# GpSimd clears 32 instead of 128 columns of `iota_i` behind each paced row gather

## The chip, the cores and the metric

One core of a Trainium2 chip runs the whole program in one launch. The metric is device time in microseconds (us). TensorE is called PE in the profile, its weight loads PEld, VectorE is DVE, ScalarE is ACT, GpSimd is POOL, and SP is the engine that only issues DMAs.

## The reference, cut to what matters

Two layers over `x` (16 sequences of 256 tokens of 256 features). Layer 0 is an attention and a feed-forward net of 8 experts, of which each token takes one. Layer 1 is a mixture of 8 small experts, of which each token takes two, plus a shared expert; then a second gated layer, in which each sequence takes two experts of 8:

```
y_all = einsum('etm,emh->eth', gp * up, w_down)        # every expert for every token
y_sel = y_all[topk_idx, arange(T)[:, None], :]         # the two that the token chose
y     = (y_sel * topk_w[..., None]).sum(1) + p         # p: the shared expert
...
pooled = y.mean(axis=1); logits = pooled @ gate_w.T + gate_b      # one set per sequence
gates  = softmax(two highest logits)
out    = x + sum over the two experts of gates * gelu(y @ expert_w.T + expert_b)
```

The kernel computes only the experts that were chosen. It sorts the 2 x 4096 (token, choice) pairs by expert into 71 tiles of 128 rows, runs each tile through its expert, writes the results to `y2_sorted` in HBM in sorted order, and then fetches for each token its two result rows.

## The kernel before, in words

The program runs in stages, and each engine has its own instruction stream; they meet at semaphores. Rows are fetched by index with `gather_rows` (line 886): GpSimd executes an indirect DMA (DMA_INDIRECT in the profile) that fetches 128 rows of 1 KB into a tile of SBUF. All gathers are GpSimd's, in the order of its stream.

Behind some gathers stands `space()` (lines 913 to 916): GpSimd clears the tile `iota_i` (128 partitions x 128 int32; it was read long before, at the start, by lines 1940 and 1941, and isn't read again), raises the semaphore `paced` and waits for it. Such a gather is called paced here. With these inputs they are:

- 16 gathers of `y_late` in `expert_rows` (lines 918 to 925), which bring layer 0's expert results to `add_rows` on VectorE (line 2563); TensorE works on the shared expert of layer 1 meanwhile (lines 1412 and 1422)
- the first 6 of the 71 gathers of `choice_rows` (lines 946 to 951), which bring the tokens of the sorted tiles. From the fourth on each also waits until TensorE has turned the tile three before it (`c_g`). TensorE turns tile `i` at line 1485 and runs it through its expert at lines 1493, 1501 and 1507
- the 64 gathers of the last stage (lines 959 to 965): four for each sequence `b` (two halves of its 256 tokens, two choices), into `yk[b % 3]`. Before the four of sequence `b` GpSimd waits until VectorE has summed sequence `b - 3` (`d_z`)

What follows in the last stage, for each sequence: VectorE sums the shared expert's row and the two fetched ones (`sum_choices`, line 2695, four instructions for a sequence, which need all four gathers landed); TensorE turns the sum (`turn_z`, line 1538); ScalarE copies it out (line 1874); TensorE makes the gate's logits (line 1546); VectorE finds the two experts (lines 2704 to 2710); TensorE runs them (lines 1553 and 1559); ScalarE applies the gelu (line 1887); VectorE adds the two results with their gates (`weigh`, line 2727, one instruction for each expert); SP stores. The order is written out by hand: in `gated_step(b)` TensorE turns `z` of `b`, works on the experts of `b - 1` around the logits of `b`, and starts on `b`'s first expert. VectorE takes the gate of `b`, the first `weigh` of `b - 1`, the sum of `b + 1`, and then the second `weigh` of `b - 1`.

Of the kernel before, what the change touches and what calls it, by code (L numbers as in the profile page):

```python
# [3 lines left out]
def bass_adaln_ffn_kernel(  # L4
# [18 lines left out]
    P = 128  # L23
# [36 lines left out]
    with ctx:  # L60
        def sb(name, shape, dt=F32):
            return ctx.enter_context(nc.sbuf_tensor(name, shape, dt))

        def sem(name):
            return ctx.enter_context(nc.semaphore(name))
# [26 lines left out]
        iota_i = sb("iota_i", [P, P], I32)  # L92
# [461 lines left out]
        paced = sem("paced")  # L554
# [242 lines left out]
        def _(pool):  # L797
# [114 lines left out]

            def space():
                spaced[0] += 1
                pool.memset(iota_i[:, :], 0).then_inc(paced, 1)  # L915
                pool.wait_ge(paced, spaced[0])

            def expert_rows(rows, first):
                for i in range(first, NC):
                    c = UNIT_CHUNKS[i]  # L920
                    if i >= first + NU:
                        pool.wait_ge(a_x1, i - NU + 1)
                    gather_rows(yg[i % NU], rows, pos_i[:, c:c + 1], a_got[i % NU // 4])
                    if first:
                        space()
# [20 lines left out]
            def choice_rows(i):  # L946
                if i >= RT:
                    pool.wait_ge(c_g, i - RT + 1)
                gather_rows(c_gath[i % RT], x1_dram, row_tok2[:, i:i + 1], c_got[i % RT])
                if i < 2 * RT:  # L950
                    space()
# [7 lines left out]
            for b in range(B):  # L959
                if b >= RT:  # L960
                    pool.wait_ge(d_z, b - RT + 1)
                for n in range(NB):
                    for k in range(2):
                        gather_rows(yk[b % RT][:, 2 * n + k, :], y2_dram, pos_k_i[:, b * NB + n, k:k + 1], d_got[b % RT])
                        space()
# [1901 lines left out]
```

## Time and profile before

| | us |
|---|---|
| median of 3 runs (lowest to highest) | 617.16 (613.28 to 618.48) |
| the profiled execution, whole | 610.94 |
| its span | 609.1 |
| busy: PE / PEld / DVE / ACT / POOL | 537.2 / 456.9 / 324.4 / 232.0 / 245.1 |
| DMA_INDIRECT of line 886, last stage (x64) | 64.6 |
| MEMSET of line 915 (x86) | 18.8 |

The span runs from the first to the last instruction of one profiled execution; whatever lies around it makes up the 1.84 us to that execution's own time. A busy share says how long an engine executed, not whether anybody waited for it. Whether an engine sets the time in a stretch is read from the chain that ended last and from the waits. Instructions of an engine are listed with start and duration; an "idle before" names what released the instruction. In every stretch that matters here TensorE had its full clock, 2.4 GHz (PEclk 1.00).

### The profile page before, as it was taken

The numbers are of one execution on the slowest core, as the hardware profiler recorded it, in microseconds if no ns is written. First come the engines' busy times: TensorE is split into PE (matmuls) and PEld (weight loads), VectorE is DVE, ScalarE is ACT, GpSimd is POOL, SyncE is SP. The second block draws the span as 40 slices with busy tenths as digits, with TensorE's granted clock in tenths as the row PEclk, the third lists the DMA queues.
The fourth block names the chain that finished last, engine by engine and source line by source line (L and its number), as shares of the span: only waits on it lengthen the run. The fifth ranks groups of instructions, "written<-read, shape, count | busy, mean of one in ns | idle before, by whom it ended". The sixth has DMA issues, their size and how long they took to land.

```text
span 609.1 us, 11343 instructions
## 1 busy us (share of the span) xinstructions
PE 537.2 (88%) x3716; PEld 456.9 (75%) x3716; DVE 324.4 (53%) x970; ACT 232.0 (38%) x651; POOL 245.1 (40%) x394
## 2 busy tenths in 40 slices
PE   0499999772499999999999999999999988988885
PEld 0478888661499999998878887888888877756564
DVE  3567667749322332772527934444444444655655
ACT  0145445550011111114554335555555454433342
POOL 6313113004211112103835446555555157877860
PEclk9999999995599999999999999999999999999999
DMA  7960000059496552341469004565656423555552
GB/s 169 357 278 2 2 2 1 2 207 415 156 341 222 181 174 53 106 136 48 93 203 300 1 25 132 157 162 154 161 154 159 112 71 121 182 158 179 166 181 72
DMA packets 53204, 88.27 MB, mean 145 GB/s; under 512 B 11250, under 2 KB 43891, under 8 KB 51604
## 3 DMA queue, kind: packets, MB, share of 16 engines
q1 hardware_dynamic: 45028, 65.29, 30.8%
q0 software_dynamic: 8112, 22.16, 15.3%
q8 instruction: 36, 0.59, 0.4%
q14 instruction: 28, 0.23, 0.1%
HBM read 62.38 MB, written 25.04 MB: 144 GB/s over the span
## 4 chain that ended last, share of the span: by engine, by line
PE 67%; POOL 13%; issue 6%; DVE 6%; DMA 5%; ACT 1%; SPq 0%; DVEq 0%; POOLq 0%; ACTq 0%
POOL arena L886 10%; PE psum L1257 10%; PE psum L1268 9%; PE psum L1493 8%; PE psum L1412 7%; PE psum L1132 5%; PE psum L1104 5%; PE psum L1507 5%; PE psum L1422 3%; DMA arena<-x,row_tok 3%; PE psum L1485 2%; POOL iota_i L915 2%; PE psum L1112 2%; PE psum L1440 1%; PE psum L1126 1%
## 5 line engine op out<-in xcount | busy, mean ns | idle before, releaser
L886 POOL DMA_INDIRECT arena<-x,row_tok x71 | 68.1, 959 | 51.3 <-PE psum L1485 44.2
L886 POOL DMA_INDIRECT arena<-y_sorted,pos_k_i x64 | 64.6, 1010 | 36.1 <-POOL iota_i L915 18.6
L1493 PE MATMUL psum<-big_w,arena 128*128 x284 | 72.9, 379 | 0.0
L1257 PEld LDWEIGHTS psum<-arena,big_w 128*128 128x128 f32 x512 | 61.4, 197 | 2.8 <-issue 1.2
L1257 PE MATMUL psum<-arena,big_w 128*128 128x128 f32 x512 | 61.8, 281 | 1.5 <-DVE arena L2441 1.5
L1559 PE MATMUL psum<-big_w,arena 128*128 x256 | 62.9, 379 | 0.0
L1780 ACT ACTIVATE arena<-psum,arena 128x128 f32<-128x128 f32 x64 | 18.2, 368 | 117.3 <-PE psum L1257 117.3
L1412 PE MATMUL psum<-arena,big_w 128*128 128x256 f32 x256 | 60.0, 381 | 0.0
L1493 PEld LDWEIGHTS psum<-big_w,arena 128*128 128x128 f32 x284 | 53.7, 190 | 7.2
L1268 PE MATMUL psum<-arena 128*128 128x256 f32 (+1 forms) x256 | 57.7, 379 | 0.0
L2678 DVE SCALAR_TENSOR_TENSOR arena<-arena 128x128 f32<-128x128 f32 x71 | 20.8, 293 | 60.7 <-ACT arena L1866 60.7
L1412 PEld LDWEIGHTS psum<-arena,big_w 128*128 128x128 f32 x256 | 47.1, 191 | 6.5 <-issue 0.4
L1268 PEld LDWEIGHTS psum<-arena 128*128 128x128 f32 x256 | 47.5, 190 | 5.8
L1559 PEld LDWEIGHTS psum<-big_w,arena 128*128 128x128 f32 x256 | 46.6, 189 | 5.6
L886 POOL DMA_INDIRECT arena<-h_late,row_tok x16 | 15.4, 960 | 85.2 <-PE psum L1245 72.7
L874 POOL TENSOR_TENSOR arena<-arena 128x512 f32<-128x512 f32 x16 | 19.0, 1189 | 65.0 <-DVE arena L2064 65.0
L1507 PE MATMUL psum<-big_w,arena 128*128 x142 | 44.0, 392 | 0.7 <-ACT arena L1863 0.7
L2695 DVE SCALAR_TENSOR_TENSOR arena<-arena,w_k 128x256 f32<-128x256 f32 x64 | 28.2, 481 | 13.1 <-issue 7.9
L1863 ACT COPY arena<-psum 128x256 f32<-128x256 f32 x71 | 26.4, 372 | 22.0 <-PE psum L1507 22.0
L1132 PE MATMUL psum<-arena 128*128 128x256 f32 x144 | 32.7, 380 | 1.6 <-ACT arena L1674 1.6
L1104 PE MATMUL psum<-arena 128*128 128x128 f32 x256 | 31.8, 285 | 0.3 <-DVE arena L2064 0.3
L1422 PE MATMUL psum<-big_w,arena 128*128 128x256 f32 x128 | 30.6, 382 | 1.3 <-ACT arena L1803 1.3
(320 smaller groups left out, 970.4 us busy)
## 6 DMA issues: line engine op xcount, KB each, us to landing
y_sorted<-arena SPq DMA_DIRECT2D x71, 128.0 KB, 2.6
big_w<-w SPq DMA_DIRECT2D x8, 1024.0 KB, 4.9
tokens<-x SPq DMA_DIRECT2D x4, 1024.0 KB, 14.0
x<-tokens SPq DMA_DIRECT2D x16, 256.0 KB, 2.9
z_kept<-arena SPq DMA_DIRECT2D x16, 256.0 KB, 3.1
out<-arena SPq DMA_DIRECT2D x16, 256.0 KB, 2.5
y_late<-arena SPq DMA_DIRECT2D x16, 128.0 KB, 1.7
big_w<-expert_w_t SPq DMA_DIRECT2D x1, 2048.0 KB, 7.6
```

Source lines behind the costliest of these rows:

```text
L886: pool.indirect_dma_start(dst, None, rows, bass.IndirectOffsetOnAxis(ap=idx, axis=0)).then_inc(done, 16)
L1104: mm = pe.matmul(bank[a][:, (j % 4) * P:(j % 4 + 1) * P], wq_s[:, k, j * P:(j + 1) * P], xt_l[:, k, :], start=k == 0, stop=k == KD - 1)
L1132: mm = pe.matmul(bank[6][:, 0:D], lhs(j), wo_s[:, j, :], start=j == 0, stop=j == NPAIR - 1)
L1257: mm = pe.matmul(bank[1 + 2 * u + f // 4][:, (f % 4) * P:(f % 4 + 1) * P], big_w[:, c:c + P], g_t[:, k, :], start=k == 0, stop=k == KD - 1)
L1268: mm = pe.matmul(bank[5 + j % 2][:, 0:D], act_t[j % 2][:, f, :], arena[:, bass.ds(e * (NF * D) + f * D, D)], start=f == 0, stop=f == NF - 1)
L1412: mm = pe.matmul(bank[up_bank(b) + q][:, half * S:(half + 1) * S], w[:, k, q * M1:(q + 1) * M1], p_s[:, unit(b)[1][k], :], start=k == 0, s ...
L1422: mm = pe.matmul(bank[6][:, n * D:(n + 1) * D], mid[u][q][:, n * P:(n + 1) * P], md_s[:, E1 + q, :], start=q == 0, stop=q == NSH - 1)
L1493: mm = pe.matmul(bank[2 + i % RT][:, 0:2 * M1], c_gt[i % RT][:, k, :], mgu_s[:, k, bass.ds(e, 1), :].rearrange("p a m -> p (a m)"), start= ...
L1507: pe.matmul(bank[5][:, 0:D], c_midt[i % RT], md_s[:, bass.ds(e, 1), :].rearrange("p a d -> p (a d)"), start=True, stop=True).then_inc(c_dn, 1)
L1559: mm = pe.matmul(o, z_t[u][:, k, n * P:(n + 1) * P], ew_s[:, k, bass.ds(e, 1), :].rearrange("p a d -> p (a d)"), start=False, stop=n == NB ...
L1863: act.copy(c_y[t % RT], bank[5][:, 0:D]).then_inc(c_yc, 1)
L2695: m = dve.scalar_tensor_tensor(z_s[u][:, n, :], yk[u][:, 2 * n + k, :], w_k[:, k, bass.ds(b * NB + n, 1)], base, ALU.mult, ALU.add)
```

## The change

`space()` clears the first `P // 4` = 32 columns of `iota_i` on all 128 partitions, not all 128 columns. The number of gathers, of clears, of semaphore steps and waits stays as it was; nothing else is changed.

```diff
             def space():
                 spaced[0] += 1
-                pool.memset(iota_i[:, :], 0).then_inc(paced, 1)
+                pool.memset(iota_i[:, 0:P // 4], 0).then_inc(paced, 1)
                 pool.wait_ge(paced, spaced[0])
```

## Rows read from the trace of the kernel before

**Rows 1.** The page: span, and the chain that ended last, by engine and line.
```profile
span 609.1 us, 11343 instructions
...
PE 67%; POOL 13%; issue 6%; DVE 6%; DMA 5%; ACT 1%; SPq 0%; DVEq 0%; POOLq 0%; ACTq 0%
POOL arena L886 10%; PE psum L1257 10%; PE psum L1268 9%; PE psum L1493 8%; PE psum L1412 7%; PE psum L1132 5%; PE psum L1104 5%; PE psum L1507 5%; PE psum L1422 3%; DMA arena<-x,row_tok 3%; PE psum L1485 2%; POOL iota_i L915 2%; PE psum L1112 2%; PE psum L1440 1%; PE psum L1126 1%
```

**Rows 2.** Busy time by stretch: start:end, length, engines' busy us, PEclk, DMA share, GB/s.
```profile
283.00:307.00 24.00, 24.00 (x156) 19.99 (x155) 10.37 (x27) 15.10 (x39) 18.97 (x32) 1.00 0.39 86
...
369.50:475.00 105.50, 105.13 (x571) 89.02 (x571) 49.15 (x189) 60.98 (x190) 60.98 (x64) 1.00 0.59 158
492.00:590.00 98.00, 85.21 (x425) 64.90 (x424) 58.10 (x183) 40.77 (x132) 77.54 (x127) 1.00 0.51 154
```

**Rows 3.** The chain that ended last, its end: start, us, what.
```profile
589.60 3.24 DMA arena<-y_sorted,pos_k_i
...
593.90 0.89 DVE arena L2695 x2
```

**Rows 4.** POOL's instructions in order of time, last stage: start, us, instruction, [idle before].
```profile
492.21 0.94 POOL L886 DMA_INDIRECT arena<-y_sorted,pos_k_i  x1 [15.93 <-DMA y_sorted<-arena]
...
522.34 1.15 POOL L886 DMA_INDIRECT arena<-y_sorted,pos_k_i  x1 [0.27 <-POOL iota_i L915]
...
531.03 1.46 POOL L886 DMA_INDIRECT arena<-y_sorted,pos_k_i  x1 [0.52 <-POOL iota_i L915]
...
536.38 0.95 POOL L886 DMA_INDIRECT arena<-y_sorted,pos_k_i  x1 [0.27 <-POOL iota_i L915]
...
573.37 0.95 POOL L886 DMA_INDIRECT arena<-y_sorted,pos_k_i  x1 [0.27 <-POOL iota_i L915]
574.32 0.22 POOL L915 MEMSET iota_i<- 128x128 int32 x1
574.81 0.95 POOL L886 DMA_INDIRECT arena<-y_sorted,pos_k_i  x1 [0.27 <-POOL iota_i L915]
...
583.70 1.04 POOL L886 DMA_INDIRECT arena<-y_sorted,pos_k_i  x1 [0.27 <-POOL iota_i L915]
...
589.60 1.21 POOL L886 DMA_INDIRECT arena<-y_sorted,pos_k_i  x1 [0.27 <-POOL iota_i L915]
```

**Rows 5.** POOL's groups by shape: line, operation, shape, count | busy us, mean ns | idle.
```profile
L915 POOL MEMSET iota_i<- 128x128 int32 x86 | 18.8, 218 | 0.1
...
L813 POOL MEMSET units<- 128x8 int32 x70 | 2.5, 94 | 0.0
...
L799 POOL MEMSET ones<- 128x128 f32 x1 | 0.2, 204 | 0.0
...
L803 POOL MEMSET router_g<- 128x64 f32 x1 | 0.1, 141 | 0.0
```

**Rows 6.** PE's instructions in order of time: start, us, instruction, [idle before].
```profile
369.49 0.44 PE L1485 MATMUL psum<-ident,arena 128*128 128x128 f32 x2 [0.27 <-DMA arena<-x,row_tok]
...
511.48 0.60 PE L1538 MATMUL psum<-ident,arena 128*128 128x128 f32 x4
...
522.72 0.66 PE L1538 MATMUL psum<-ident,arena 128*128 128x128 f32 x4
...
528.08 0.66 PE L1538 MATMUL psum<-ident,arena 128*128 128x128 f32 x4
...
595.76 0.66 PE L1538 MATMUL psum<-ident,arena 128*128 128x128 f32 x4 [1.21 <-DVE arena L2695]
```

**Rows 7.** DVE's instructions in order of time: start, us, instruction, [idle before].
```profile
530.93 0.73 DVE L2727 SCALAR_TENSOR_TENSOR arena<-arena,tokens 128x512 f32<-128x512 f32 x1
...
581.33 1.79 DVE L2695 SCALAR_TENSOR_TENSOR arena<-arena,w_k 128x256 f32<-128x256 f32 x4 [0.42 <-issue]
...
587.41 1.80 DVE L2695 SCALAR_TENSOR_TENSOR arena<-arena,w_k 128x256 f32<-128x256 f32 x4 [0.64 <-issue]
...
589.24 0.74 DVE L2727 SCALAR_TENSOR_TENSOR arena<-arena 128x512 f32<-128x512 f32 x1
```

## The prediction

> **What bounds the kernel now.** I read the page's chain first: POOL has 13% of it, nearly all of it line 886 with 10% and line 915, the clears, with 2% [rows 1]. So the clears are on the path somewhere, and the question is where. The table by stretch tells it [rows 2]. While the 16 paced gathers of layer 0's results run (283 to 307 us), PE is busy for 24.00 of 24.00 us: GpSimd isn't what is late. In the sorted tiles PE is busy for 105.13 of 105.5 us. In the last stage (492 to 590 us) PE drops to 85.21 of 98 us while POOL shows 77.54 us busy, and most of POOL's remaining 20 us is the 0.27 us that it idles between each clear and the gather behind it [rows 4]. POOL therefore has no free time of its own there: gather, clear, wait for the clear, gather. The end of the chain says the same [rows 3]: the last gather starts at 589.60, its rows and the step from them to VectorE take until 593.90, the sum of the last sequence follows, and the last turn on PE starts at 595.76 after 1.21 us of idling for that sum [rows 6]. From there to the end of the span are 13.3 us of work that the change doesn't touch.
>
> How far PE is behind is the bound on any gain. Two turns with no idling before the second lie 5.36 us apart (522.72 and 528.08) [rows 6]; that is PE's own step for a sequence. The turn of sequence 1 is at 511.48, that of sequence 15 at 595.76: 84.28 us for 14 steps, 6.02 a step. At 5.36 a step the last turn would stand at 586.5, 9.2 us earlier. POOL's own pace: first gather 492.21, last (the 64th) 589.60, so 63 distances in 97.39 us, 1.546 each, or 6.18 for a sequence of four. POOL is the slower of the two, by 0.82 us a sequence.
>
> **The change part by part.** Only the clear's length changes, 86 times. A clean distance between gathers is 574.81 - 573.37 = 1.44 us: 0.95 for the gather, 0.22 for the clear, 0.27 for the clear's release of the next gather [rows 4]. The first and the last of these I leave as they are: the same count of instructions, the same semaphore, the same wait.
>
> No clear of 32 columns of this tile is in the trace, so its price is bounded. GpSimd clears 128x8 in 94 ns, 128x64 in 141 ns and 128x128 in 204 ns (float) or 218 ns (this line) [rows 5]. From 8 to 128 int32 columns that is 124/120 = 1.03 ns a column, and 32 columns would take 94 + 24 x 1.03 = 119 ns; over the pair 8 and 64 it is 0.84 ns a column and 114 ns. The shortest that it can be is about the 94 ns of 8 columns; the longest, from 64 columns, 141 ns plus the 14 ns by which this line is above the float clear, 155 ns. So the saving lies between 63 and 124 ns a gather; I take 98 ns (218 - 120), since 8 and 64 columns agree on it to 6 ns.
>
> The Trainium skill ("GPSIMD Engine Reference", section 3.1, the cycle accounting) has a floor of 1.03 cycles an element for the simplest loops. At 1.2 GHz 96 columns would be 82 ns by it, and the last stage's term below 5.2 us instead of 6.2; the rows here show a somewhat steeper slope, so the rows decide.
>
> Last stage: the last gather has 63 clears ahead of it, 63 x 0.098 = 6.2 us earlier (4.0 to 7.8 by the bounds). The landing and the sum follow it, and nothing else stands between: the cap of 9.2 us isn't reached, though it is near. What is late next is PE's own step, 5.36 us, against a sequence of gathers at 6.18 - 0.39 = 5.79 us. GpSimd's wait for `d_z` has room: gathers of `b` wait for the sum of `b - 3`, which is some two sequences old by then.
>
> Sorted tiles: six clears, of which four stand ahead of the fifth gather; PE idles 0.27 us for that gather's rows before its turn at 369.49 [rows 6], and from there to 475 it is full [rows 2]. 4 x 0.098 = 0.39 us earlier would remove that 0.27 us and no more: 0.3 us, which the later PE-bound stretch passes on (0 to 0.4).
>
> Layer 0's results: 16 clears x 0.098 = 1.6 us earlier for the last of 16 gathers. I cost it at nothing: PE's shared-expert matmuls cover it, with no idle time in 24 us [rows 2]. Without that cover it would be worth those 1.6 us.
>
> Sum: 6.2 + 0.3 = 6.5 us, from 610.94 (span 609.1 and 1.84 around it) to 604.4 for the profiled execution. The median of the runs, 617.16, is 6.2 above this execution, which was faster than all three runs; I take the difference off the median: **610.7 us**.
>
> **The rivals.**
>
> *Collisions eat a part (614).* Not every gather takes 0.95 us. The one at 531.03 took 1.46 and ended at 532.49; VectorE's `weigh` had started just before it, at 530.93, and ended at 531.66 [rows 4, 7]. The one at 589.60 took 1.21 and ended at 590.81; its `weigh` ran from 589.24 to 589.98. Both end 0.83 us behind the end of VectorE's instruction: a gather that starts while it runs is held until it is done. This makes a trap for the change. The second `weigh` stands directly behind a sum of 1.8 us, and the last gather of the next sequence starts about there, 583.70 being 2.37 behind the sum's start at 581.33; it ended 3.41 behind it, and the next sum came at 587.41, 2.67 after that: 6.08 for the sequence. A gather that starts earlier within the same `weigh` ends at the same point, so the shorter clear gives nothing. A sequence would be held at about 3.41 + 2.67 = 6.08 us. Against the mean of 6.18 that is 0.1 on each of some ten sequences, and the full 0.39 on the first five, where GpSimd runs ahead of VectorE: 1 + 2 = 3 us, 614.2. The held gathers speak for it; against it, that a gather that comes before the `weigh` begins isn't held at all, and shorter distances carry more gathers past it.
>
> The Trainium skill ("SBUF — State Buffer", section "Who interferes with whom") has this as a rule: a VectorE instruction with two SBUF inputs and a GpSimd instruction that reads SBUF exclude each other, and the one that starts first keeps the shared port until it is done. Both `weigh` and the sum have two SBUF inputs, and a gather reads its indices; by that rule the two long gathers above are what one would see, and the trace agrees.
>
> *PE becomes the bound (608).* If more gathers slip ahead of VectorE's instructions than before, the excess shrinks too: 1.546 - 1.44 = 0.11 us a gather, 6.7 us in all. Then POOL would need 5.4 us a sequence, PE's step of 5.36 takes over, and the gain is the cap: 9.2 + 0.3 = 9.5 us, 607.7.
>
> *Slower (624).* The new distances could fall in with VectorE badly throughout. The worst stretch before is 522.34 to 536.38, eight distances in 14.04 us, 1.755 each [rows 4], an excess of 0.32. With 0.098 off and that excess all along, 63 x 1.657 = 104.4 us against 97.4: 7.0 us slower, less the 0.3 of the sorted tiles, 623.9. It decides from a mean excess of 0.11 + 0.10 = 0.21 us on. Against it: the excess is mostly of VectorE's making, a fixed set of instructions for a sequence, and the later stretch from 536.38 to 589.60 (35 distances in 53.22 us, 1.52 each) has 0.08.
>
> *The clear isn't shorter (617).* If a fixed cost ruled, or if the wait behind it grew as it shrank, nothing would move. The 94 ns of 8 columns speaks against the first; no row speaks on the second.
>
> **How the numbers follow.** Chances: the forecast 0.50 (own range 608.5 to 613), collisions 0.24, PE the bound 0.14, no shorter 0.07, slower 0.05. About 1% (6.2 us) is what a measurement of this kernel tells from no change, and the forecast of 6.5 lies at that edge. Faster by over 1%: 0.30 of the forecast's 0.50, and all of the 0.14, with a little for the runs' own spread of 5 us: 0.46. Slower by over 1%: 0.04. The rest is within 1%: 0.50. The range reaches from the cap, 607.5, over the forecast and the collision case to 616.0; out of it are the case without effect, the slower one and a few strays.
>
> **What would show each step.** The clear's row at 112 to 128 ns and still 86 of them; clean distances of 1.34 us in the last stage, 0.27 us of idling behind the clear as before; first gather to last in about 91 us instead of 97.4; the last turn some 6 us earlier, and idling of PE before `turn_z` in fewer steps but not gone; about 13.3 us from that turn to the end. The tile stage's 0.27 us gone, and the stretch from 283 to 307 as full as it was. The collision case would show gathers of 1.2 to 1.5 us behind `weigh` in most sequences and steps of 6.1 us. PE as the bound would show turns 5.36 us apart with no idling before them, and GpSimd waiting for `d_z`. The prediction is wrong if the clear takes over 155 ns, if the wait behind it is no longer 0.27 us, or if the mean excess of a gather moves from 0.11 us by more than 0.05.

## The result, and the profile after

The changed kernel took 630.64 us (median of 4 runs, 629.01 to 634.57) against 616.31 us for the kernel before (4 runs, 613.28 to 618.48): 14.3 us slower. The ratio is 1.026 with the interval 1.0219 to 1.0302; it isn't taken from the medians, whose quotient is 1.023. The profiled execution took 632.22 us with a span of 630.4. I had forecast 610.7 us, faster instead of slower, and the result is far above the range's end of 616.0.

The page of the kernel after: its span, and the chain that ended last by engine.
```profile
span 630.4 us, 11343 instructions
...
PE 76%; DVE 7%; issue 5%; ACT 4%; DMA 3%; another core or an unknown queue 3%; POOL 1%; SPq 0%; DVEq 0%; ACTq 0%; POOLq 0%
```
POOL has gone from 13% of the chain to 1% [rows 1]. GpSimd is off the path, but not because its clears are short: where the same kernel isn't slowed (e9_after_third, below), POOL keeps 12% of the chain. What came in its place is work of the other engines, and 3% (about 19 us) whose releaser the profile can't name.

The clears by shape, kernel after (columns as in [rows 5]), and the same three stretches as in [rows 2]:
```profile
L915 POOL MEMSET iota_i<- 128x32 int32 x86 | 11.9, 138 | 0.1
```
```profile
283.00:307.00 24.00, 15.86 (x99) 12.63 (x101) 6.66 (x18) 9.69 (x26) 17.86 (x32) 0.88 0.38 88
369.50:475.00 105.50, 104.37 (x563) 87.64 (x562) 51.03 (x191) 59.38 (x184) 61.12 (x69) 1.00 0.55 147
492.00:590.00 98.00, 83.83 (x405) 65.20 (x404) 49.81 (x160) 40.09 (x128) 64.52 (x113) 0.97 0.45 139
```
The clear is shorter, 138 ns instead of 218. But in the first stretch, where PE was full before, it is now busy 15.86 of 24 us, VectorE and ScalarE do less too, and PE's granted clock is 0.88 instead of 1.00 in the mean. The DMA's share (0.38 against 0.39) and the GB/s (88 against 86) are as before, so these two means show no crowding of the transfers. The middle stretch, with GpSimd mostly waiting for PE between its gathers, is hardly touched. The third is the same stretch of time but not of work, since by then this kernel is 11.6 us late; the events below are the better measure.

GpSimd's own rows, kernel after, in order of time (columns as in [rows 4]): the first gather of the sorted tiles, the first of the last stage, a clean pair, and the last gather. The kernel before's own first gather of the sorted tiles stands ahead of them.
```profile
360.06 1.18 POOL L886 DMA_INDIRECT arena<-x,row_tok  x1 [4.54 <-DVE row_tok L2640]
```
```profile
371.12 1.18 POOL L886 DMA_INDIRECT arena<-x,row_tok  x1 [4.55 <-DVE row_tok L2640]
...
503.79 0.94 POOL L886 DMA_INDIRECT arena<-y_sorted,pos_k_i  x1 [16.30 <-DMA y_sorted<-arena]
...
574.25 0.95 POOL L886 DMA_INDIRECT arena<-y_sorted,pos_k_i  x1 [0.27 <-issue]
575.21 0.14 POOL L915 MEMSET iota_i<- 128x32 int32 x1
575.62 0.95 POOL L886 DMA_INDIRECT arena<-y_sorted,pos_k_i  x1 [0.27 <-POOL iota_i L915]
...
600.49 0.95 POOL L886 DMA_INDIRECT arena<-y_sorted,pos_k_i  x1 [0.27 <-POOL iota_i L915]
```
And the turns of the last sequences on PE:
```profile
584.21 0.66 PE L1538 MATMUL psum<-ident,arena 128*128 128x128 f32 x4 [0.41 <-issue]
...
595.23 0.62 PE L1538 MATMUL psum<-ident,arena 128*128 128x128 f32 x4
...
606.17 0.60 PE L1538 MATMUL psum<-ident,arena 128*128 128x128 f32 x4
611.47 0.65 PE L1538 MATMUL psum<-ident,arena 128*128 128x128 f32 x4
616.82 0.66 PE L1538 MATMUL psum<-ident,arena 128*128 128x128 f32 x4
```
The two profiles stand 21.3 us of span apart, more than the 14.3 of the medians: the profiled execution of the kernel before was 5.4 us faster than the median of its runs. By the mark that the last section names (landing times on the page) it comes from an occasion of the faster kind, and the result from one of the slower. No trace of the kernel before from a slower occasion is there to set beside it; the nearest is e7_choice6, whose time stayed, and whose events (first gather of the tiles 359.39, of the last stage 492.42, last turn 596.11) are within 0.7 us of those of the kernel before. Where the 21.3 us went can be read off against the same events before. The first gather of the last stage moved from 492.21 [rows 4] to 503.79, 11.58 later: nearly all of it was lost ahead of the sorted tiles, whose first gather is at 371.12 (360.06 before). The last gather moved from 589.60 to 600.49, 10.89 later, so GpSimd gained 0.7 us in the last stage. The last turn moved from 595.76 [rows 6] to 616.82, 21.06 later: 16.3 us behind the last gather instead of 6.2. So half of the loss arose in the first stage (11.1 us) and half in the last (9.5), and not in the gathers' own pace in either. In the last stage the sequences fell behind gathers that were on time. Two steps that were 5.35 and 5.85 us before take 11.02 and 10.94 here (584.21 to 595.23 to 606.17), and so does an early one (523.44 to 534.49, 11.05 us instead of 5.93); once the gathers are over, PE goes at 5.30 to 5.35 a step again.

What a step lost looks like on the engines. First stage, kernel after: PE's matmuls of the router's logits, and ScalarE's copy of them (L1832), which waits for nothing but these matmuls and its own previous instruction.
```profile
287.77 1.07 PE L1395 MATMUL psum<-arena,router_g 128*32 128x256 f32 x16
```
```profile
288.30 0.62 ACT L1799 COPY arena<-psum 128x512 f32<-128x512 f32 x1
291.69 0.37 ACT L1832 COPY arena<-psum 128x256 f32<-128x256 f32 x1 [2.77 <-remote]
294.69 0.38 ACT L1811 ACTIVATE arena<-psum 128x256 f32<-128x256 f32 x1 [2.62 <-remote]
...
300.35 0.58 ACT L1803 COPY arena<-psum 128x512 f32<-128x512 f32 x1 [3.71 <-remote]
```
The matmuls end at 288.84, ScalarE is free at 288.92, and the copy starts at 291.69, 2.85 us after the one and 2.77 after the other. "remote" says that the trace holds no event that ended the wait. Last stage, the same on VectorE: its first instruction on the logits of the choice, behind PE's matmuls.
```profile
526.62 0.61 PE L1546 MATMUL psum<-big_w,arena 128*128 128x8 f32 x4 [1.72 <-ACT arena L1874]
```
```profile
531.44 0.17 DVE L2704 SCALAR_TENSOR_TENSOR arena<-psum,arena 128x8 f32<-128x8 f32 x1 [10.29 <-remote]
```
The logits are there at 527.23 and VectorE takes them at 531.44, 4.2 us later. Between them GpSimd's gathers go on every 1.36 us, the last of them from 530.48 to 531.43. Then GpSimd itself stands still for 3.62 us, since it waits for VectorE's next sum: the late engine holds up the gathers in turn.

A late start costs PE its clock as well. Its turn at 534.49 stands behind an idle time of 3.65 us, took 1.12 us where the ones above took 0.60 to 0.66, and the granted clock from 534.5 to 535.5 was 0.50, which is the lower of TensorE's two levels, 1.2 GHz:
```profile
532.84 0.39 PE L1553 MATMUL psum<-big_w,ones_bf 128*128 x1 [3.65 <-issue]
...
534.49 1.12 PE L1538 MATMUL psum<-ident,arena 128*128 128x128 f32 x4
```
Over the whole program PE was busy for 545.8 us, against 537.2 before, with the same instructions.

### The profile page after: what moved, and what is told of

Same layout as the page of the kernel before. It is cut to its first block, busy times and chain, and to the rows that moved or that the text cites. A ratio compares the mean times of both kernels' runs of the same rounds, so it can differ in the third digit from the quotient of the medians.

```text
span 630.4 us, 11343 instructions
## 1 busy us (share of the span) xinstructions
PE 545.8 (87%) x3716; PEld 462.5 (73%) x3716; DVE 322.9 (51%) x970; ACT 232.2 (37%) x651; POOL 238.8 (38%) x394
## 4 chain that ended last, share of the span: by engine, by line
PE 76%; DVE 7%; issue 5%; ACT 4%; DMA 3%; another core or an unknown queue 3%; POOL 1%; SPq 0%; DVEq 0%; ACTq 0%; POOLq 0%
PE psum L1257 9%; PE psum L1493 9%; PE psum L1268 9%; PE psum L1412 7%; PE psum L1559 6%; PE psum L1132 5%; PE psum L1507 5%; PE psum L1104 5%; PE psum L1422 4%; PE psum L1485 2%; PE psum L1112 1%; PE psum L1546 1%; PE psum L1538 1%; ACT arena L1874 1%
## 5 line engine op out<-in xcount | busy, mean ns | idle before, releaser
L886 POOL DMA_INDIRECT arena<-y_sorted,pos_k_i x64 | 64.9, 1014 | 40.3 <-DMA y_sorted<-arena 16.3
L1493 PE MATMUL psum<-big_w,arena 128*128 x284 | 72.9, 379 | 0.0
L1559 PE MATMUL psum<-big_w,arena 128*128 x256 | 68.0, 402 | 0.0
L1493 PEld LDWEIGHTS psum<-big_w,arena 128*128 128x128 f32 x284 | 53.7, 190 | 7.2
L1559 PEld LDWEIGHTS psum<-big_w,arena 128*128 128x128 f32 x256 | 50.2, 203 | 7.5 <-issue 0.2
L1268 PEld LDWEIGHTS psum<-arena 128*128 128x128 f32 x256 | 47.5, 190 | 5.8
L1507 PE MATMUL psum<-big_w,arena 128*128 x142 | 44.1, 392 | 0.7 <-ACT arena L1863 0.7
L1422 PE MATMUL psum<-big_w,arena 128*128 128x256 f32 x128 | 31.9, 394 | 1.9 <-ACT arena L1803 1.9
L1132 PEld LDWEIGHTS psum<-arena 128*128 128x128 f32 x144 | 26.7, 190 | 5.9 <-issue 2.4
## 6 DMA issues: line engine op xcount, KB each, us to landing
y_sorted<-arena SPq DMA_DIRECT2D x71, 128.0 KB
y_late<-arena SPq DMA_DIRECT2D x16, 128.0 KB, 1.7
```

The lines of the kernel that those rows point to most:

```text
L886: pool.indirect_dma_start(dst, None, rows, bass.IndirectOffsetOnAxis(ap=idx, axis=0)).then_inc(done, 16)
L1132: mm = pe.matmul(bank[6][:, 0:D], lhs(j), wo_s[:, j, :], start=j == 0, stop=j == NPAIR - 1)
L1268: mm = pe.matmul(bank[5 + j % 2][:, 0:D], act_t[j % 2][:, f, :], arena[:, bass.ds(e * (NF * D) + f * D, D)], start=f == 0, stop=f == NF - 1)
L1422: mm = pe.matmul(bank[6][:, n * D:(n + 1) * D], mid[u][q][:, n * P:(n + 1) * P], md_s[:, E1 + q, :], start=q == 0, stop=q == NSH - 1)
L1493: mm = pe.matmul(bank[2 + i % RT][:, 0:2 * M1], c_gt[i % RT][:, k, :], mgu_s[:, k, bass.ds(e, 1), :].rearrange("p a m -> p (a m)"), start= ...
L1507: pe.matmul(bank[5][:, 0:D], c_midt[i % RT], md_s[:, bass.ds(e, 1), :].rearrange("p a d -> p (a d)"), start=True, stop=True).then_inc(c_dn, 1)
```

## The experiments

Eighteen runs on five chips. The kernels on one chip share its runs of the kernel before. One table first, since only all of them together tell the story ("distance" is the clean distance of two paced gathers where the edit applies; "16", "6" and "64" are the gathers of layer 0's results, of the sorted tiles and of the last stage). As in the result, the ratio isn't taken from the medians.

| run | clear | distance, us | chip | us | before | ratio, interval |
|---|---|---|---|---|---|---|
| (result) | 32, all | 1.36 | first | 630.64 | 616.31 | 1.026, 1.0219 to 1.0302 |
| e1_first16 | 32, the 16 | 1.36 | 13 | 611.95 | 612.14 | 0.9994, 0.9978 to 1.001 |
| e2_last64 | 32, the 64 | 1.36 | 13 | 606.50 | 612.14 | 0.9902, 0.9881 to 0.9922 |
| e3_cols64 | 64, all | 1.39 | 13 | 608.25 | 612.14 | 0.9935, 0.9909 to 0.9961 |
| e4_none | none | 1.25 | 13 | 601.36 | 612.14 | 0.9819, 0.98 to 0.9838 |
| e5_after_again | 32, all | 1.36 | 2 | 628.02 | 613.62 | 1.0237, 1.0205 to 1.027 |
| e6_16and64 | 32, 16 and 64 | 1.36 | 2 | 628.52 | 613.62 | 1.0241, 1.0197 to 1.0285 |
| e7_choice6 | 32, the 6 | 1.36 | 2 | 612.89 | 613.62 | 0.9993, 0.9974 to 1.0011 |
| e8_cols16 | 16, all | 1.35 | 2 | 631.26 | 613.62 | 1.0258, 1.0206 to 1.0311 |
| e9_after_third | 32, all | 1.36 | 8 | 607.75 | 612.35 | 0.9937, 0.992 to 0.9954 |
| e10_first16_again | 32, the 16 | 1.36 | 8 | 611.88 | 612.35 | 1.0007, 0.9986 to 1.0027 |
| e11_last64_again | 32, the 64 | 1.36 | 8 | 608.15 | 612.35 | 0.9927, 0.9901 to 0.9953 |
| e12_cols64_again | 64, all | 1.39 | 8 | 608.60 | 612.35 | 0.9952, 0.9933 to 0.9972 |
| e13_after_fourth | 32, all | 1.36 | 11 | 630.85 | 615.54 | 1.0259, 1.0208 to 1.0309 |
| e14_first16_third | 32, the 16 | 1.36 | 11 | 625.74 | 615.54 | 1.0174, 1.0128 to 1.022 |
| e15_last64_third | 32, the 64 | 1.36 | 11 | 622.63 | 615.54 | 1.012, 1.0084 to 1.0155 |
| e16_none_again | none | 1.25 | 11 | 646.27 | 615.54 | 1.0486, 1.0395 to 1.0577 |
| e17_two_short | 32 and 8, all | 1.40 | 3 | 609.14 | 611.04 | 0.9961, 0.9944 to 0.9978 |
| e18_cols64_third | 64, all | 1.39 | 3 | 609.10 | 611.04 | 0.9952, 0.9924 to 0.9979 |

One of e11's six executions took 3101.91 us. The ratio leaves it out, the median of 608.15 us has it in (608.04 without it), and no trace shows what happened there.

**Chip 13: which of the gathers cost, and how it goes with the distance.** The edits:
```
 def space(cols=P):
-    pool.memset(iota_i[:, :], 0).then_inc(paced, 1)
+    pool.memset(iota_i[:, 0:cols], 0).then_inc(paced, 1)
...
+    space(P // 4)          # e1: in layer 0's results; e2: in the last stage
```
```
-    pool.memset(iota_i[:, :], 0).then_inc(paced, 1)
+    pool.memset(iota_i[:, 0:P // 2], 0).then_inc(paced, 1)     # e3
```
```
 def space():
-    spaced[0] += 1
-    pool.memset(iota_i[:, :], 0).then_inc(paced, 1)
-    pool.wait_ge(paced, spaced[0])
+    pass                                                      # e4
```

> 32 columns only behind the 16 gathers of layer 0's results, 128 behind the other 70. Rate theory (gathers that follow each other at 1.36 us instead of 1.44 us make the other engines start late after their semaphores): the 16 gathers alone bring the 11 us that the first stage lost, so 1.018 of the time before (+11 us, 9 to 13). Rival, chance alignment of that one program from the start on: within 1% of before, or anything else.

> 32 columns only behind the 64 gathers of the last stage. Rate theory: the last stage alone loses what it lost with the whole change, about 9 us of the 20: ratio 1.012 to 1.018, and ScalarE and VectorE wait for 'remote' or 'issue' in that stage. Rival, the loss of the last stage is only inherited from the first: 5 us faster than before (64 clears, 80 ns each), ratio 0.992.

> 64 columns behind all 86 gathers. The clear should take about 165 ns and the distance of gathers 1.39 us. Rate theory: a loss between those at 1.44 us (none) and 1.36 us (16 to 20 us), say +8 us with all between 0 and +20 possible, since it depends on where the edge lies. Rival, the loss belongs to 32 columns as such: 3 us faster than before.

> No clear and no wait behind any gather; distances of 1.25 us, as the unpaced ones in the trace of before. Rate theory: at least as slow as with 32 columns, +16 to +30 us. Rival, the short clear with its semaphore step and wait makes the loss, not the rate: faster than before by up to the cap of PE's own step, 9 us.

Measured: nothing for the 16 (0.9994), 1.0% faster for the 64, 0.65% faster with 64 columns, 1.8% faster with no clear at all. None of the loss of the result was to be seen, neither its half of the first stage nor that of the last. The row of the first stretch with no clear, e4_none:
```profile
283.00:307.00 24.00, 24.00 (x155) 20.01 (x154) 10.22 (x27) 14.97 (x39) 15.94 (x16) 1.00 0.39 89
```
It is full, with gathers 1.25 us apart. Either the three edits together did something that none did alone, or the same code behaves differently on another occasion. The changed kernel itself isn't among these, so they can't tell the two apart.

**Chip 2: the changed kernel again, with and without the 6.** `space(P // 4)` behind the 16 and the 64 (e6), in the sorted tiles alone (e7), and `0:P // 8` at all (e8).

> The changed kernel again, unaltered, beside the kernel before on one chip. Theory A (the loss belongs to the program: the parts don't add up because the six gathers of the sorted tiles or the combination matter): about 1.026 again, with ScalarE and VectorE waiting for 'remote' in its trace. Rival B (the stalls belong to an occasion or to one chip, not to the program): about 0.989 here, 6 to 7 us faster, as the sum of the parts.

> 32 columns behind the 16 and behind the 64 gathers, 128 behind the 6 of the sorted tiles. Theory A with the six gathers as cause: 0.990 (6 us faster). Theory A with the combination of 16 and 64 as cause: 1.02. Rival B: 0.990.

> 32 columns only behind the first 6 gathers of the sorted tiles. Theory A with these as cause: slower, up to 1.02. Rival B: same, at most 0.3 us faster.

> 16 columns behind all 86 gathers, distance about 1.34 us. If the time follows the distance of the gathers in the last stage: 0.987 to 0.990, between 32 columns there (6 us faster) and no clear at all (11 us faster). If short clears on all 86 gathers bring the stalls: 1.02 or more.

The loss was back: 1.0237 for the changed kernel, 1.0241 without the 6, nothing for the 6 alone (0.9993), 1.0258 with 16 columns. So the 6 play no part. That left the two readings of chip 13 open, since no kernel but the one before had run on both chips.

**Chip 8: the changed kernel beside its two parts.** e10, e11 and e12 repeat the edits of e1, e2 and e3.

> The changed kernel once more. So far the runs with 32 columns behind the 16 alone or the 64 alone were on one occasion and not slowed, and those with both on another occasion and slowed by 14 us. Theory C (the occasion, not the program, brings the stalls to any program with short clears): this and the next two are all slowed (1.02) or all not (0.989). Theory A (the pair of 16 and 64 brings them): this one 1.024, the next two as before.

> 32 columns behind the 16 only, again. Theory A: same as before (0.999). Theory C, on an occasion on which the changed kernel is slowed: slowed as well, by the part that the first stage lost, 5 to 11 us (1.008 to 1.018).

> 32 columns behind the 64 only, again. Theory A: 0.990. Theory C, on an occasion on which the changed kernel is slowed: 1.00 to 1.02.

> 64 columns behind all, again. Theory A: 0.9935 again, since the distance of 1.39 us isn't short enough. Theory C with a sensitivity to any shorter distance: slowed, 1.00 to 1.02. Theory C with an edge between 1.36 and 1.39 us: 0.9935.

The changed kernel is *faster* here, 0.9937, as its part of 64 is (0.9927), its part of 16 is nothing (1.0007), and 64 columns give 0.9952. Not a combination then: one and the same code takes 607.75 us on this occasion and 628.02 on that of chip 2. I call occasions like this one quiet, and those on which the loss shows slowing. The same two rows as above, of e9_after_third, and its three stretches:
```profile
287.83 1.07 PE L1395 MATMUL psum<-arena,router_g 128*32 128x256 f32 x16
```
```profile
288.97 0.37 ACT L1832 COPY arena<-psum 128x256 f32<-128x256 f32 x1
```
```profile
283.00:307.00 24.00, 24.00 (x155) 20.07 (x154) 10.44 (x28) 15.19 (x39) 17.92 (x32) 1.00 0.40 89
369.50:475.00 105.50, 104.81 (x570) 89.05 (x570) 49.27 (x189) 61.04 (x189) 60.93 (x64) 1.00 0.60 158
492.00:590.00 98.00, 88.28 (x441) 67.53 (x439) 59.27 (x189) 42.83 (x140) 75.08 (x128) 1.00 0.53 161
```
The matmuls end at 288.90 and the copy starts at 288.97: 0.07 us, where it was 2.85. The gathers and clears are the same ones, at the same 1.36 us.

**Chip 11: is it the rate of the gathers, and do the parts add up?** The changed kernel, its two parts, and no clear at all, so that on a slowing occasion the distances 1.44, 1.36 and 1.25 would stand side by side.

> The changed kernel, to tell the occasion: 1.02 to 1.03 on a slowing one, 0.989 to 0.994 on another. No theory so far says which it will be.

> 32 columns behind the 16 only. On a slowing occasion, theory C: about 1.01 (the 5 to 11 us of the first stage); theory A (only the pair of 16 and 64 is slowed): 1.00. On another: 1.00.

> 32 columns behind the 64 only. On a slowing occasion, theory C: 1.00 to 1.02, the stalls of the last stage alone; theory A: 0.990. On another: 0.990.

> No clears. On a slowing occasion, theory C with the distance as cause: 1.02 or more, since 1.25 us is shorter still; theory C with only distances near 1.35 us affected: 0.982. On another: 0.982.

It was a slowing one. The 16 alone cost 10.2 us (1.0174, more than the 1.01 expected) and the 64 alone 7.1; both together 15.3, so the two parts nearly add up, and theory A is out. Without any clear, the kernel that was the fastest on chip 13 is the slowest of all: 646.27 us, 1.0486. Loss against distance: 15.3 us at 1.36, 30.7 at 1.25. By stage the traces tell more. Against the kernel before, the first gather of the sorted tiles is 12.5 us late in e13_after_fourth and 12.8 in e16_none_again; from the first gather of the last stage to the last turn they take 7.1 and 24.2 us longer. So the larger loss without clears is all in the last stage. The rows of e16_none_again, first stretch and last, and ScalarE's copy of the logits in it (its lines stand 2 lower) behind the matmuls that release it:
```profile
283.00:307.00 24.00, 16.03 (x90) 12.61 (x88) 6.08 (x16) 8.09 (x22) 15.33 (x16) 0.93 0.39 88
...
492.00:590.00 98.00, 74.21 (x339) 57.64 (x339) 40.28 (x128) 33.67 (x108) 48.19 (x48) 0.90 0.39 117
```
```profile
287.13 1.07 PE L1393 MATMUL psum<-arena,router_g 128*32 128x256 f32 x16
```
```profile
292.56 0.37 ACT L1830 COPY arena<-psum 128x256 f32<-128x256 f32 x1 [4.28 <-remote]
```
And a longer late start in the last stage, ScalarE's on products that PE had ready at 518.26, 10.2 us before, also e16_none_again:
```profile
514.64 3.62 PE L1410 MATMUL psum<-arena,big_w 128*128 128x256 f32 x16
```
```profile
528.50 0.38 ACT L1809 ACTIVATE arena<-psum 128x256 f32<-128x256 f32 x1 [9.08 <-remote]
```
The copy of the logits is 4.36 us late here, against 2.85 at 1.36 us; on the quiet chip 13 without clears it was 0.07 (289.15 to 289.22). This run also tells what doesn't do it: it has no clear and no increment of `paced`, so neither the clears nor their semaphore is needed for the loss. What is left of GpSimd's work in these stages is the gathers.

Two more rows, the first stretch of e14_first16_third (1.36 us in it) and of e15_last64_third (1.44 us in it, as before):
```profile
283.00:307.00 24.00, 17.33 (x95) 13.78 (x93) 6.09 (x16) 8.76 (x23) 17.66 (x32) 0.88 0.38 88
```
```profile
283.00:307.00 24.00, 22.20 (x142) 17.84 (x141) 9.12 (x24) 12.42 (x32) 18.46 (x32) 1.00 0.38 88
```
Even the kernel's own 1.44 us isn't free of it on this chip: 22.20 of 24 us, and in the last stage of e14_first16_third, with 1.44 us as before, VectorE takes one sequence's logits 2.8 us late. That fits the kernel before, whose medians are 611.0 to 612.4 us on the three quiet occasions and 613.6 to 616.3 on the three slowing ones.

**Chip 3: the distance or the length of the clear?** Two short clears were to make up the old distance with a 32-column clear in it. They made 1.40 us, not the 1.45 to 1.50 expected, so this kernel doesn't quite hold the old distance. One wait stands for both, and 64 columns stand beside it (e18). The edit of e17:
```
-    spaced[0] += 1
-    pool.memset(iota_i[:, :], 0).then_inc(paced, 1)
+    spaced[0] += 2
+    pool.memset(iota_i[:, 0:P // 4], 0).then_inc(paced, 1)
+    pool.memset(iota_i[:, P // 4:P // 4 + 8], 0).then_inc(paced, 1)
     pool.wait_ge(paced, spaced[0])
```

> Behind each gather two short clears, of 32 and of 8 columns, with one wait for both: about 0.14 + 0.09 us, so a distance of about 1.45 to 1.50 us, no shorter than before. If the distance of the gathers makes the loss: 1.000 to 1.006 on any occasion, no wait for 'remote'. If the short clear does: 1.02 or more on a slowing one.

> 64 columns behind all, distance 1.39 us. On a slowing occasion, if the loss grows with the rate (1.44 us none, 1.36 us 2.5%, 1.25 us 4.9%): about 1.00 to 1.02. On another: 0.9935 to 0.995.

The occasion was quiet: 0.9961 and 0.9952. It says only that the faster side goes with the distance too: 1.9 us gained at 1.40 and at 1.39. The two clears overlap, so that a pair costs about 40 ns more than the one of 32 columns. e17_two_short, GpSimd in order of time:
```profile
578.09 0.95 POOL L886 DMA_INDIRECT arena<-y_sorted,pos_k_i  x1 [0.27 <-POOL iota_i L916]
579.04 0.14 POOL L915 MEMSET iota_i<- 128x32 int32 x1
579.10 0.12 POOL L916 MEMSET iota_i<- 128x8 int32 x1
579.49 1.00 POOL L886 DMA_INDIRECT arena<-y_sorted,pos_k_i  x1 [0.27 <-POOL iota_i L916]
```
The question that these two runs were for is still open, since it can only be asked on a slowing occasion.

## Why the prediction was wrong, by its own steps

**The clear's price.** 138 ns, not the 120 that I took, and within the bounds of 94 and 155. The mistake was to draw the line from the 94 ns of 8 columns, which are a clear of another tile (`units`) at another place of the program. Clears of `iota_i` measured 165 ns with 64 columns (e3), 126 with 16 (e8) and 118 with 8, there as the second of a pair (e17). From 128 to 64 that is 0.83 ns a column, from 64 to 32 0.84, and the line through 128 and 64 gives 138 for 32. The saving was 80 ns, not 98, and the clean distance 1.36, not 1.34. The floor of the Trainium skill ("GPSIMD Engine Reference", section 3.1) gave an estimate of 82 ns for the 96 columns; here the page was nearer than the line through my rows, and with it the term of the last stage would have been 5.2 us.

**The last stage, -6.2 us.** On the quiet occasion of e9_after_third the step held, with the size off: the median came down by 4.6 us, not 6.5. Its last turns on PE, and VectorE's second `weigh` of those sequences, and the gathers that start inside it:
```profile
567.76 0.66 PE L1538 MATMUL psum<-ident,arena 128*128 128x128 f32 x4
573.87 0.66 PE L1538 MATMUL psum<-ident,arena 128*128 128x128 f32 x4 [0.82 <-DVE arena L2695]
580.01 0.66 PE L1538 MATMUL psum<-ident,arena 128*128 128x128 f32 x4 [0.84 <-DVE arena L2695]
586.12 0.65 PE L1538 MATMUL psum<-ident,arena 128*128 128x128 f32 x4 [0.81 <-DVE arena L2695]
```
```profile
573.86 0.74 DVE L2727 SCALAR_TENSOR_TENSOR arena<-arena 128x512 f32<-128x512 f32 x1
...
579.99 0.74 DVE L2727 SCALAR_TENSOR_TENSOR arena<-arena 128x512 f32<-128x512 f32 x1
...
586.10 0.74 DVE L2727 SCALAR_TENSOR_TENSOR arena<-arena 128x512 f32<-128x512 f32 x1
```
```profile
574.14 1.29 POOL L886 DMA_INDIRECT arena<-y_sorted,pos_k_i  x1 [0.27 <-POOL iota_i L915]
...
580.27 1.29 POOL L886 DMA_INDIRECT arena<-y_sorted,pos_k_i  x1 [0.27 <-POOL iota_i L915]
...
586.38 1.29 POOL L886 DMA_INDIRECT arena<-y_sorted,pos_k_i  x1 [0.27 <-POOL iota_i L915]
```
63 x 0.080 = 5.0 us were to be had, and the last gather came 3.5 us earlier against the first (93.91 us for 63 distances instead of 97.39); the mean excess rose from 0.11 to 0.13 us. The end shows the trap of the collision rival: a gather in each sequence ends 0.83 us behind the end of `weigh` (586.38 + 1.29 = 587.67, and 586.10 + 0.74 = 586.84), and the turns lie 6.11, 6.14 and 6.11 us apart, where the rival said 6.08. So on a quiet occasion the truth lay between the forecast's 6.5 us and that rival's 3. The rule of the Trainium skill named there ("SBUF — State Buffer", "Who interferes with whom") agrees with these rows.

On the occasion of the result, the stage cost 9.5 us instead (21.06 less 11.58). This is **the step that failed**: "The landing and the sum follow it, and nothing else stands between". The sum priced a shorter distance by GpSimd's own path alone. What a gather does to the others was priced by one mechanism, the collision of `weigh` with a gather, and the lower bound of this term was a gain of 4.0 us. The only rival with a loss, *Slower*, priced GpSimd's path again. No loss on the other engines' side was bounded, although nothing in the trace excluded one: it holds no two paced gathers closer than 1.44 us.

**Layer 0's results, nothing.** "PE's shared-expert matmuls cover it": true on the quiet occasions (24.00 of 24 us; e1 0.9994, e10 1.0007). On the slowing ones this step failed as well: the term was put at nothing, and the stage cost 11.06 us in the result, and shorter clears in it alone made the run 10.2 us longer (e14). The cover hides a gain of GpSimd's; it doesn't hide a loss that falls on the covering engines. A full PE has no room for a late start of the engines that feed it, so here each of them shows in the time.

**Sorted tiles, -0.3 us.** Too small for the runs to tell: the 6 alone gave 0.9993, with an interval of 0.9974 to 1.0011. The trace doesn't show the gain: the fifth turn idles 0.80 us in e9_after_third, where the kernel before had 0.27.

**The other rivals.** *PE the bound* came true where the clear is gone altogether (e4, quiet): turns 5.35 us apart at the end, and 10.8 us faster, past the 9.5 that the rival gave it. *Slower* gave a time (624) not far from the slowing runs, but by another mechanism: it asked for a mean excess of over 0.21 us a gather, and in the result it was 0.17 (96.70 us for 63 distances; a move of 0.06, just past the 0.05 that the prediction names as a sign of being wrong). The gathers of the last stage took 0.7 us less than before, not more. So that rival had the sign and not the cause. *The clear isn't shorter* fell with the first row: 138 ns, and the idling behind it still 0.27 us.

**What the cause is, and how far it is shown.** Shown: on three of six occasions, engines begin work 1 to 10 us after their wait's producer is done while paced gathers run; in the result's trace ScalarE and VectorE end ten idle times of over 1.5 us with "remote", in those of e9_after_third, e4_none, e7_choice6 and the kernel before none. The loss comes with a shorter distance in either stage alone (e14, e15, beside the kernel before on the same chip). Over the whole program it is next to none or a few us at 1.44 us, 2.4 to 2.6% at 1.36, and 4.9% at 1.25; the step from 1.36 to 1.25 rests on one kernel and on its last stage. And the clears or their semaphore aren't needed for it (e16). A second part of it is PE's clock: the granted clock was 0.88 in the stretch from 283 to 307 and 0.97 from 492 to 590, 0.90 there without clears, with 0.50 in the row behind a late start above. Not shown: which part of the chip passes the semaphores late. That the gathers' own completions crowd out other engines' semaphores is the reading that I find likeliest, and it is an inference; no run measured it by itself. The Trainium skill ("VectorE: DVE Perf Modes", the section on the TRN2 errata) warns that on trn2 one kind of semaphore increment, at a high rate from one engine, can deadlock another, and that kernels with dense increments on completion from multiple engines should space them. Nothing locked up in any run here; a wait that ends microseconds late is a milder thing, and no run tells whether it is the same one.

Open too: chip or occasion. Every chip was used on one occasion only, so the two can't be separated. A rival that no run tests is the recording: every time here comes from an execution whose span and clock were recorded, and each slowed trace lacks part of its events (the last section has the numbers). e7_choice6 lacks them too and isn't slowed, so missing events alone aren't the loss; that recording and close gathers together bring it isn't excluded. Whether the clear protects by its length or by the distance that it makes, and what 64 columns do on a slowing occasion, was to be measured on chip 3, and that occasion was quiet.

For the choice of a version: without clears it is the best where it is quiet (0.9819) and the worst where it isn't (1.0486). No version was shown to be better on both; 128 columns is the one whose cost is known on both.

## What to carry to other kernels

A short dummy instruction behind a DMA that GpSimd issues may be a spacer, and its price has two sides: time on GpSimd's path, and what the closer gathers do to engines that wait for each other's semaphores. When a change raises the rate of such gathers beyond any in the trace, bound its cost on the side of a loss too, above all in stretches where another engine "covers" it, and run the changed kernel on more than one chip before believing either sign: here one gave 0.994, another 1.026.

## What the runs showed of the hardware that I had not expected

- The same program is 20 to 23 us apart between occasions (607.75 on chip 8; 628.02, 630.64 and 630.85 on three others), while the kernel before, with 1.44 us between gathers, is 5 us apart (611.0 to 616.3).
- The traces of slowing occasions hold fewer events (about 5900 to 6300 semaphore updates, against 8060 to 8230 in the others): the page's row `y_sorted<-arena SPq DMA_DIRECT2D x71, 128.0 KB` has no landing time there, where quiet ones have 2.5 or 2.6 us. e7_choice6, whose time wasn't touched, has the same gap (611.79 us in its profile). So it marks the occasion and not the loss; but no trace with a loss is without it.
- GpSimd's clears of `iota_i` have a fixed part and a slope: 126 ns for 16 columns (e8), 138 for 32, 165 for 64 (e3), 218 for 128 [rows 5]. With the clear and its wait taken out altogether, the distance falls only to 1.25 us (e4), since 0.30 us of idling remains between one gather and the next. So the 0.27 us that the prediction read as the clear's release of the next gather isn't the clear's: the wait for the clear costs nothing beyond the clear's own time.
